# Spacing one engine's indirect transfers differently: attention's row sends, the last batch's sends, and the gathers of returned rows

## The reference, cut to what matters

```python
x = x + attention(layernorm(x))     # 16 heads, low-rank queries and keys, causal softmax
x = x + moe(layernorm(x))           # 64 experts, top 6 per token, plus a shared expert
x = x + ssd(layernorm(x))           # Mamba-2 scan: conv, gates, chunkwise states
x = x + ffn(layernorm(x))           # 704 hidden, ternary weights, gate_s, up_s, down_s scales

# moe: combine weights from the top 6 router probabilities
routed_out = jnp.einsum('teh,te->th', y, combine)
# ffn: the last product is scaled by column
out = jnp.einsum('ti,hi->th', hdn, down_w) * down_s
```

## Time and profile before

| | us |
|---|---|
| time, median of 3 runs | 1321.08 (1320.51 to 1321.24) |
| profiled execution, span | 1372.1 |
| profiled execution, own time beside its span | none is given apart from the span |
| PE busy | 1236.2 (90%) |
| DVE busy | 801.9 (58%) |
| ACT busy | 463.7 (34%) |
| POOL busy | 376.6 (27%) |

### The profile page before, as it was taken

One profiled execution on the slowest core, in us unless ns is written; L12 is line 12 of the kernel. 1 busy time (PEld: TensorE's weight loads), 2 busy tenths in 40 slices (PEclk: granted clock), 3 DMA queues, 4 the chain that ended last, 5 costly groups with the idle time before them and its releaser, 6 DMA issues.

```text
span 1372.1 us, 19483 instructions
## 1 busy us (share of the span) xinstructions
PE 1236.2 (90%) x6005; PEld 767.3 (56%) x6005; DVE 801.9 (58%) x2226; ACT 463.7 (34%) x1057; POOL 376.6 (27%) x464
## 2 busy tenths in 40 slices
PE   6999999989999899988959999997585987999988
PEld 3566566555555466556536777775244545555454
DVE  6377767786578667784513434334665673685431
ACT  2455435442455335442201111111331612625310
POOL 1242023451425413351340000113564261311200
PEclk9799999999999999999979999999777998999999
DMA  9999999999800100010336888884212021000000
GB/s 320 413 419 420 420 421 420 420 420 418 334 1 32 62 1 1 8 58 30 107 103 191 274 263 269 270 278 138 67 43 62 1 70 39 12 12 16 0 16 16
DMA packets 89422, 235.48 MB, mean 172 GB/s; under 512 B 12768, under 2 KB 23680, under 8 KB 89088
## 3 DMA queue, kind: packets, MB, share of 16 engines
q1 hardware_dynamic: 70912, 192.54, 37.9%
q0 software_dynamic: 9216, 25.18, 5.8%
q10 hardware_dynamic: 9216, 16.78, 3.2%
HBM read 66.70 MB, written 167.77 MB: 171 GB/s over the span
## 4 chain that ended last, share of the span: by engine, by line
PE 72%; DVE 15%; issue 4%; another core or an unknown queue 3%; ACT 2%; SPq 2%; DMA 1%; POOL 1%; ACTq 0%; DVEq 0%; POOLq 0%
PE bank L521 6%; PE bank L547 5%; PE bank L480 4%; PE bank L609 4%; PE bank L530 4%; PE bank L481 4%; PE bank L1327 4%; PE bank L1349 3%; PE bank L1588 3%; PE bank L1594 3%; DVE negmax L853 3%; PE bank L1605 3%; DVE r L864 2%; PE bank L1639 2%
## 5 line engine op out<-in xcount | busy, mean ns | idle before, releaser
L700 ACT ACTIVATE r<-bank,negmax 128x128 f32<-128x128 f32 (+3 forms) x256 | 134.9, 527 | 173.7 <-DVE negmax L853 163.5
L521 PE MATMUL bank<-r 128*128 128x512 f32 (+3 forms) x512 | 184.2, 443 | 0.0
L853 DVE TENSOR_REDUCE negmax<-bank 128x1 f32<-128x128 f32 (+3 forms) x256 | 124.1, 485 | 55.9 <-PE bank L522 53.0
L530 PE MATMUL bank<-tables,r 128*128 128x128 f32 x640 | 117.7, 284 | 19.8 <-DVE r L864 18.6
L964 POOL TENSOR_TENSOR r<-r,tables 128x256 f32<-128x256 f32 x56 | 42.0, 749 | 331.7 <-ACT r L681 331.6
L1198 POOL DMA_INDIRECT sent<-r,slots x96 | 93.9, 978 | 113.0 <-ACT r L700 49.1
L530 PEld LDWEIGHTS bank<-tables,r 128*128 128x128 f32 x640 | 75.2, 145 | 74.6 <-issue 35.6
L1436 DVE COPY r<-bank 128x512 f32<-128x512 f32 x64 | 41.2, 685 | 116.3 <-PE bank L1358 75.3
L864 DVE TENSOR_SCALAR r<-r,rrow 128x128 f32<-128x128 f32 (+3 forms) x256 | 103.8, 406 | 0.3
L521 PEld LDWEIGHTS bank<-r 128*128 128x128 f32 x512 | 77.8, 191 | 23.6 <-issue 18.4
L1214 POOL DMA_INDIRECT r<-sent,slots x16 | 15.2, 950 | 223.3 <-DMA sent<-r 219.6
(11 more groups left out here) (276 smaller groups left out, 2404.4 us busy)
## 6 DMA issues: line engine op xcount, KB each, us to landing
sent<-gath SPq DMA_DIRECT2D x8, 16384.0 KB, 88.1
r<-waT_dram SPq DMA_DIRECT2D x64, 304.0 KB, 3.1
r<-sent SPq DMA_DIRECT2D x64, 256.0 KB
sent<-r ACTq DMA_DIRECT2D x64, 256.0 KB
w2buf<-wcT_dram SPq DMA_DIRECT2D x64, 48.0 KB, 3.5
r<-w_o_dram SPq DMA_DIRECT2D x1, 2048.0 KB, 11.2
sent<-gath SPq DMA_DIRECT2D x2, 1024.0 KB, 56.7
out_dram<-x SPq DMA_DIRECT2D x4, 512.0 KB, 2.9
```

What stands on the lines that cost most here:

```text
L521: nc.tensor.matmul(at[:, 0:n], QT[g % 2][:, h, i * P:(i + 1) * P], KT[:, 0:n], start=True, stop=False)
L530: last = nc.tensor.transpose(bank[TRANS[u % 2]][:, j * P:(j + 1) * P], prob[:, u % 4, j * P:(j + 1) * P], ident)
L700: nc.scalar.activation(prob[:, u % 4, 0:(i + 1) * P], bank[SCORE[u % 4]][:, 0:(i + 1) * P], ACT.Exp, bias=negmax[:, u:u + 1], scale=1.0, a ...
L853: nc.vector.tensor_reduce(negmax[:, u:u + 1], bank[SCORE[u % 4]][:, 0:(i + 1) * P], axis=AX.X, op=ALU.max, negate=True).then_inc(A["max"], 1)
```

## The change

Three things change, all of them in POOL's list. No instruction of computation or transfer is added or removed; two waits per scan batch are new (in the two batches that have such gathers) and four waits on `A["exp"]` per attention batch go.

1. In attention, each `turn` of head group 3 is followed by three sends and not two (12 and not 8), and in head group 3 the sends that wait for units are 12 and not 16: behind units 1, 3, 5, 7 and 8 to 15.
2. For the last batch, two scale products stand behind every eighth send, and the wait for the weights (`loaded(pool, "ffn1")`) stands ahead of the first send.
3. At the end of a scan batch, the second tile's gathers wait for PE's last `output` of this batch, and the third tile's for the end of the next batch's `branch`.

```diff
-                            send(b - 1, 2 * i)
-                            send(b - 1, 2 * i + 1)
+                            for m in range(3):
+                                send(b - 1, 3 * i + m)
                 if b:
                     g = GROUPS * b + GROUPS - 1
-                    for u in range(NU):
+                    for m, u in enumerate((1, 3, 5, 7, *range(8, NU))):
                         pool.wait_ge(A["exp"], NU * g + u + 1)
-                        send(b - 1, 2 * TB + u)
+                        send(b - 1, 3 * TB + m)
...
-        def scale_down(pool):
-
-            for c, (lo, w) in enumerate(FF_CHUNKS):
+        def scale_down(pool, chunks):
+
+            for c in chunks:
+                w = FF_CHUNKS[c][1]
...
                 if b + 2 < BATCH:
-                    for i in range(RING):
-                        return_pool(pool, n + 2 * TB + i)
+                    return_pool(pool, n + 2 * TB)
+                    pool.wait_ge(S["out"], n + TB)
+                    return_pool(pool, n + 2 * TB + 1)
+                    pool.wait_ge(S["br"], CH * (b + 2))
+                    return_pool(pool, n + 2 * TB + 2)
...
             send_ready(pool, BATCH - 1)
+            loaded(pool, "ffn1")
             for n in range(TB * TOPK):
                 send(BATCH - 1, n)
-            loaded(pool, "ffn1")
-            scale_down(pool)
+                if n % 8 == 7:
+                    scale_down(pool, range(n // 8 * 2, n // 8 * 2 + 2))
```

## The result

Both kernels ran side by side. Before: 1319.87 us, median of 6 runs (1316.16 to 1321.24). After: **1324.57 us**, median of 6 (1323.62 to 1328.32). The ratio is **1.0046, 95% interval 1.0033 to 1.0059**: the change makes the kernel 5 to 6 us slower (4.7 by the medians, 6.1 by the ratio).

What follows compares the result with a forecast made beforehand. PE was taken as the bound, 72% of the chain. The median 1321.1 us plus 2.5 for part 2 and 0 for parts 1 and 3 gave 1323.6 us, range 1304 to 1327.

Steps and rivals of the forecast that it cites:

- These pauses belong to the execution that was being recorded.: Waits beside dense indirect transfers, 46.6 us plus 6.7 us slow products, are in the profile; timed runs have few or none.
- The pauses are in every run: Rival: the timed runs hold the pauses wholly or in part; 1277 us if all 46.6 were real and went; chance 0.30.
- I charge the whole 2.5 us: Loop start after the last batch's sends: scale products delay the last send by 2.5 us (2.2 to 3.0), all charged.
- SP's side ends later: At the loop's start, SP's row loads finish some 1.5 us after PE's side, so the sends set the start.
- no cost: Attention head group 3: three sends per turn cost nothing, with 2.2 us left before PE transposes the fourth turn's queries.
- the turns come late: Rival, head group 3: PE waits about 1 us per batch for the fourth turn; about 1327 us with part 2; chance 0.04.
- cost nothing: Scan batch ends: paced gathers end at 1076 to 1078.7 us, ahead of the next batch's first `decays` at 1080.5.
- late `decays`: Rival, scan: the third six gathers hold up `decays` 6.1 us in two batches, giving 1335.8 us; chance 0.06.
- What would show it: Changed profile: pauses gone or shorter, DVE's group 3 wait in batch 3 near 2 us, span perhaps 1330, last send near 703.
- my reading of the 51 us: Span exceeds median by 51.0 us because pauses and slow products (53.3 us) sit in the recorded execution, not the timed runs.

Runs made afterwards that it cites:

- part 2 alone: The kernel before with only the second change, scale products among the last batch's sends: 1322.55 us, ratio 1.0022 to the kernel before.
- part 3 alone: The kernel before with only the third change, the scan's gathers paced in three sixes: 1319.29 us, ratio 0.9991 to the kernel before.
- before_again: The kernel before, unchanged, recorded and timed once more on a pausing chip: 1374.34 us, ratio 0.9996 to the kernel before.
- parts 1 and 3: The changed kernel with its second change undone, the six scale products again behind the 24 sends: 1322.75 us, ratio 1.0020 to the kernel before.

## Why the prediction was right, and where it was wrong

**The forecast** of 1323.6 us lies 1.0 us under the median of after, and the sign that it leaned to (2.5 us slower) is right. That it came so near is luck: it did so because the kernel before was itself 1.2 us faster in this comparison than its first three runs, against 3.4 us missing for part 1, and because the pauses were left out, for a false reason, on a chip where leaving them out was right. The loss itself was forecast at 2.5 us and measured at 5 to 6.

- *"These pauses belong to the execution that was being recorded."* Wrong in its cause. The arithmetic was right (46.6 us of pauses and 6.7 of slow products are the difference of 51), and the runs of that comparison have none of them. But they don't belong to recording: the timed runs of two other comparisons take 1374.75 and 1373.59 us. "The pauses are in every run", the first rival, is true there, in its strongest form: the gain is 40 us, where I gave 44 (1321 to 1277) to all of them gone. I had the span and the median from two sources and took it for granted that one chip stood behind both. That two did is the likeliest account, no more, as said above.
- *Part 2, "I charge the whole 2.5 us".* Right: 2.71 us between the sends, 2.3 at the loop, within the 2.2 to 3.0 given. The last send started at 692.11 and not near 703, since everything ahead of it ran without pauses; the distances hold: SP's first row load 3.35 us behind the last send's start (3.2 expected, from the earlier trace rows, which are gathers; the sends of the change land in 2.4), the second pair's 6.5 us later, the first L1327 another 5.2 behind that. "SP's side ends later" is right, but by 7.0 us, all of PE's wait for rows, and not by 1.5.
- *Part 1, "no cost".* This step failed, by 3.4 us. The look at the fourth turn was right as far as it went: a turn period of 6.2 us (574.15, 580.29, 586.49), and PE's fourth transposes wait 0.49 us for ACT with the part and 0.55 without (part 2 alone). What I left out is where the moved turns land. I costed POOL's delay by who waits for POOL; the price was paid by DVE, whose normalizations wait for nothing of POOL's in the program. The rival "the turns come late" had the size (PE about 1 us late in each of three batches) and the wrong road to it.
- *Part 3, "cost nothing".* Right: ratio 0.9991, and the first decays of the second batch are released by DVE's step sizes, with 2.86 us in hand:

```profile
1039.40 1.03 POOL L1245 DMA_INDIRECT gath<-sent,slots  x1 [0.30 <-issue]
1043.29 3.75 POOL L1551 TENSOR_TENSOR r<-tables,r 128x1024 f32<-128x1024 f32 x2 [2.86 <-DVE r L1973]
```

  The last gather ends 16.2 us behind the start of `branch` (1040.43 less 1024.21); I had said 14.5 to 17.2. The six gathers took 0.95 to 1.41 us each, so the rival of late `decays` didn't come. The Trainium skill's rule of the shared ports (SBUF — State Buffer, SBUF: two separate sides) I had weighed on the gathers alone, where its 3100 ns don't show; on the turns, where I didn't look, three rows of batch 3 fit it and others don't.
- *What would show it.* DVE's wait in group 3 of batch 3 fell from the 5.5 us of the earlier trace rows to 1.5:

```profile
DVE negmax L853 <- PE bank L522: 1.5, 1, 1.5
```

  It looks foreseen, but part 3 alone, with 16 sends there as before, has 1.6 us too: on a quiet chip the wait is short without the change. The span fell to 1322.0 and not to 1330. A fall of the span and a rise of the median looked like proof of my reading of the 51 us, and it wasn't: a pausing and a quiet chip give the same picture.

## What to carry to other kernels

Before a span is set against a median, make sure that both come from one chip and one session: record and time the kernel before once more beside the change. When POOL's elementwise work is moved in time, look at what DVE runs then, not only at who waits for POOL; an instruction of 0.34 us took 1.28 where it started 0.02 us behind one of a turn. An edit that guards against a rare or local trouble has two prices: here 0.5% on a quiet chip against 3% gained on a pausing one, and more than half of the 0.5% was had back by keeping the turns' pace (0.18% left).

## What the hardware showed that was not expected

- Two levels of one kernel, 1319 and 1374 us, most likely by chip. On the higher one engines wait up to 16 us for work long done while a row of POOL's indirect transfers runs. In `before_again` the long pause ends at 705.69, 4.9 us behind the start of the last of 24 sends (700.77). Rows of eight sends with 1.4 us of scale products between them left the start of the loop free; with one product of 0.73 us the pause was back. What makes a chip pause, and why 18 gathers bring one in some executions only, stays open.
- The scan's first batch differs by 3 us between profiles, with PE's granted clock. A stretch of 12 us in part 3 alone, 34.7 us behind the start of that batch, and the stretch at the same place of the batch in the change (columns: busy of PE, PEld, DVE, ACT, POOL, granted clock, DMA share, GB/s):

```profile
978.50:990.50 12.00, 12.00 (x14) 3.37 (x12) 9.12 (x13) 0.00 (x0) 9.12 (x8) 0.50 0.23 66
```

```profile
984.00:996.00 12.00, 9.04 (x32) 3.39 (x32) 11.42 (x15) 1.75 (x4) 10.30 (x9) 1.00 0.24 68
```

  In the first PE is granted half its clock (1.2 GHz) and busy throughout, 14 products in 12 us; in the second it has the full 2.4 GHz, and 32 products take 9.04 us. That batch takes 77.43 us with part 3 alone and 77.54 with parts 1 and 3, against 74.38 to 75.26 in the other executions on quiet chips. Timed against each other the kernels don't show these 3 us, so it may be a matter of the single execution; but the two slow ones are the two kernels with part 3 and without part 2, and the edits aren't ruled out. One profile says little about a difference of that size.
